# Tanh of a convolved x unit written into its projection's PSUM bank; the tails' B.C copies moved from VectorE to ScalarE

## The chip, the cores and the metric

The kernel runs on one core of one Trainium2 chip. The metric is the device time of one execution in microseconds (us), the median of several runs.

## The reference, cut to what matters

The reference takes x (4 batches of 256 tokens, 512 features) through half an FFN, a Mamba2 mixer, and half an FFN again, each on a layer-normalised input and added back to x. Only the mixer is touched by the change:

```python
proj = hidden_states @ in_proj_w.T
gate, xBC, dt = jnp.split(proj, [INTER, INTER + CONV_DIM], axis=-1)
conv = jax.lax.conv_general_dilated(xBC_t, conv_w, ...)          # causal, 4 taps, by channel
xBC = jax.nn.silu(jnp.swapaxes(conv + conv_b[None, :, None], 1, 2))
x, Bm, Cm = jnp.split(xBC, [INTER, INTER + NG * SS], axis=-1)
scores = jnp.einsum('bclhn,bcshn->bchls', Cc, Bc) * Lmat         # B.C times a decay
Ydiag = jnp.einsum('bchls,bcshp->bclhp', scores, xdt)
yg = y * jax.nn.silu(gate)                                       # then a group RMS norm
return out @ out_proj_w.T
```

INTER is 8192, in NG = 8 groups. A group has its own B and C (128 channels each) and eight x tiles of 128 channels.

## The kernel before, in words

The mixer works group by group (g = 0 to 7). A group has 20 **units**: a unit is one tile of 128 channels (B, C or an x tile) over one half of the 1024 tokens, so 128x512. Units 0 to 3 are B and C, units 4 to 19 the eight x tiles. Each unit passes through five stations:

1. `project` (TensorE, L164 to L166, 12 matmuls of 512 columns) leaves the projection in PSUM bank u % 2.
2. `evacuate` (ScalarE, L955) writes the last tap plus bias from the bank to `acc` in SBUF.
3. `taps` (VectorE, L970, three instructions) read the bank again, shifted, and add to `acc`.
4. `tanh_conv` (ScalarE, L1278) writes tanh of `acc` to the SBUF tile `th`.
5. `silu_conv` (VectorE, L1455) computes `acc = (th + 1) * acc`, with both inputs in SBUF, and raises the semaphore `conv`.

So the bank is free for unit u+2 once the taps of u are done, and that is what `project` waits for. Of the semaphores here, `tap` counts finished taps and `conv` finished `silu_conv`.

The order on every engine is written out by hand: one instruction stream for each, held together by semaphores. A group is eight **pairs** (j = 0 to 7) and a **tail**. In pair j TensorE runs: two transposes of x (L1648), two unit projections, two gate projections (L164 to L166 again, into other banks), two output projections (operand `mx_wo`), and two `mix_tokens` (L1675, L1679). In pair 0 the unit projections (units 6 and 7) come ahead of the transposes. In the first half of group 0 there are no output projections. The tail projects units 2 to 5 of the next group, with the B.C products (`b_dot_c`, L1636, L1637) for each half of the tokens and the sums of squares (L1706) between.

On VectorE a pair has `skip_y` (L1491), `scale_x` (L1480), two `make_mix` (L1473, a decay matrix times `cbt`), the taps of two units, their `silu_conv`, two `silu_gate` (L1497, one input in SBUF, one in PSUM), and `split_wo` (L1501). `cbt` is the SBUF copy of the B.C products. In the tails VectorE copies it (L1462, four instructions of 384 columns for a tail); for group 0 ScalarE does (L1344). GpSimd (POOL) works on SBUF tiles alongside.

Of the kernel before, what the change touches and what calls it, by code (L numbers as in the profile page):

```python
# [28 lines left out]
ALU = mybir.AluOpType  # L29
# [12 lines left out]
TAPS = 4  # L42
# [4 lines left out]
HB = HALF // SEQ  # L47
STEPS = 2 * XT
UNITS = 4 + STEPS
# [4 lines left out]
PAIR = SEQ + CH  # L54
# [767 lines left out]
def first(g):  # L822

    return isinstance(g, int) and g == 0
# [29 lines left out]
def start_at_one(eng, sems):  # L854


    for sem in sems:
        eng.sem_inc(sem, 1)
# [9 lines left out]
class InProj:  # L868
# [51 lines left out]
    def project(self, pe, g, u):  # L920
        nc, m, s = self.nc, self.m, self.s
        w, hf, _ = unit_of(u)
        pe.wait_ge(s["wlo"], 1 + WPG * g + w + 1)
        if not (first(g) and u < 2):
            pe.wait_ge(s["tap"], 1 + (TAPS - 1) * (UNITS * g + u - 1))
        at = slice(hf * HALF, (hf + 1) * HALF)
        for k in range(KT):
            last = three_pass(nc, m.bank[u % 2][:, :], self.w_hi[:, w % 3, k, :], self.w_lo[:, w % 3, k, :],
                              m.h_hi[:, k, at], m.h_lo[:, k, at], k == 0, k == KT - 1)
        last.then_inc(s["proj"], 1)  # L930
# [96 lines left out]
def mixer_phase(nc, m, ip, norm_w, w_out, ncs_dram, next_ln, sums, early):  # L1027

    with ExitStack() as ctx:
# [3 lines left out]
        s, acc, d_raw, w_hi, w_lo = ip.s, ip.acc, ip.d_raw, ip.w_hi, ip.w_lo  # L1033
# [12 lines left out]
        th = sb("th", [P, 2, HALF])  # L1046
        xd = sb("xd", [P, 2, HB * 2, 2, HD])
        mix = sb("mix", [P, 2, 2, HB, PAIR])
        cbt = sb("cbt", [P, 2, HB, PAIR])
# [17 lines left out]
        def step_slot_freed(eng, sem, g, st):  # L1067

            if not (first(g) and st == 0):
                eng.wait_ge(sem, 1 + STEPS * g + st - 1)  # L1070

        def groups_in_turn(pair, tail):

# [184 lines left out]

        @block.scalar
        def _(act):  # L1260
            start_at_one(act, [s["tg"], s["decay"], s["sq"], s["wohi"], s["gcopy"], s["root"]])
            start_after_quad(act, [s["yhi"]])

            def split_wo(g, j):
# [7 lines left out]
            def evacuate(g, u):  # L1272
                ip.evacuate(act, g, u)

            def tanh_conv(g, u):
                act.wait_ge(s["tap"], 1 + (TAPS - 1) * (UNITS * g + u + 1))
                act.wait_ge(s["conv"], 1 + UNITS * g + max(u - 1, 0))
                nc.scalar.activation(th[:, u % 2, :], acc[:, u % 4, :, :].rearrange("p b t -> p (b t)"),  # L1278
                                     ACT.Tanh).then_inc(s["th"], 1)

            def decay_from_first(g, st):

                i, j, hf = st % 2, st // 2, st % 2
                act.wait_ge(s["masked0"], 1 + STEPS * g + st + 1)
                step_slot_freed(act, s["y"], g, st)
                for b in range(HB):
                    for hd in range(2):
                        tile, head = 2 * (HB * hf + b), GH * g + 2 * j + hd
                        nc.scalar.activation(mix[:, i, hd, b, 0:SEQ], csb[:, i, hd, b * SEQ:(b + 1) * SEQ], ACT.Exp,  # L1289
                                             bias=m.ncs[:, tile, head:head + 1], scale=-1.0)  # L1290
# [45 lines left out]
                if n < NG * WPG:  # L1336
                    ip.round_w(act, *weight(n))

            def keep_bc(hf):

                act.wait_ge(s["cb"], 1 + hf + 1)
                banks = Y_BANK if hf == 0 else O_BANK
                for b in range(HB):
                    last = nc.scalar.activation(cbt[:, hf, b, :], banks[b][:, 0:PAIR], ACT.Copy)  # L1344
                last.then_inc(s["cbt"], 1)

            tanh_conv(0, 2)
            keep_bc(0)
            round_w(3)
            tanh_conv(0, 3)  # L1350
            round_w(4)
# [3 lines left out]
            tanh_conv(0, 4)  # L1355
            decay_from_second(0, 0)
            tanh_conv(0, 5)
            keep_bc(1)
            decay_from_first(0, 1)
            decay_from_second(0, 1)  # L1360

# [38 lines left out]
            def tail(g, more):  # L1400
                if more:
                    decay_from_first(g + 1, 0)
                    decay_from_second(g + 1, 0)
                    evacuate(g + 1, 2)
                    square(g, STEPS - 2)
                    round_w(WPG * (g + 1) + 3)
                    evacuate(g + 1, 3)
                    tanh_conv(g + 1, 2)
                    round_tile(g + 1, 0)
                    square(g, STEPS - 1)  # L1410
                    round_w(WPG * (g + 1) + 4)
                    tanh_conv(g + 1, 3)
                    evacuate(g + 1, 4)
                    decay_from_first(g + 1, 1)
                    evacuate(g + 1, 5)
                    tanh_conv(g + 1, 4)
                    decay_from_second(g + 1, 1)
                    round_tile(g + 1, 1)
                    tanh_conv(g + 1, 5)
                else:  # L1420
                    square(g, STEPS - 2)
                    round_tile(NG, 0)
                    square(g, STEPS - 1)
                    keep_first_quad(g, STEPS - 1)
                    for p in range(1, 4):
                        round_tile(NG, p)
                    root(g)
                    for p in range(4, 7):
                        round_tile(NG, p)
                    next_ln.root(act, 0)  # L1430
                    next_ln.normalise(act, 0)
                    next_ln.normalise(act, 1)
                    round_tile(NG, 7)
                    next_ln.normalise(act, 2)
                    next_ln.normalise(act, 3)
                    for t in range(4):
                        next_ln.round(act, t)
                    next_ln.root(act, 1)
# [2 lines left out]

        @block.vector
        def _(dve):
            start_at_one(dve, [s["mix"], s["xd"], s["sg"], s["ysb"], s["cbt"],
                               s["ms"], s["inv"], s["wolo"]])
            start_after_quad(dve, [s["gsum"], s["outsb"]])

# [3 lines left out]
            def silu_conv(g, u):  # L1451

                dve.wait_ge(s["th"], 1 + UNITS * g + u + 1)
                a = acc[:, u % 4, :, :].rearrange("p b t -> p (b t)")
                nc.vector.scalar_tensor_tensor(a, th[:, u % 2, :], 1.0, a, ALU.add, ALU.mult).then_inc(s["conv"], 1)  # L1455

            def keep_bc(g, hf):
                dve.wait_ge(s["cb"], 1 + 2 * g + hf + 1)
                dve.wait_ge(s["mix"], 1 + STEPS * g)
                banks = Y_BANK if hf == 0 else O_BANK  # L1460
                for b in range(HB):
                    last = nc.vector.tensor_copy(cbt[:, hf, b, :], banks[b][:, 0:PAIR])  # L1462
                last.then_inc(s["cbt"], 1)

            def make_mix(g, st):

# [104 lines left out]
            def tail(g, more):  # L1571
                skip_y(g, STEPS - 2)
                skip_y(g, STEPS - 1)
                if more:
                    head_constants(g + 1)
                    taps(g + 1, 2)
                    taps(g + 1, 3)
                    silu_conv(g + 1, 2)
                    silu_conv(g + 1, 3)
                    taps(g + 1, 4)  # L1580
                    taps(g + 1, 5)
                    mean_square(g)
                    silu_conv(g + 1, 4)
                    silu_conv(g + 1, 5)
                    keep_bc(g + 1, 0)
                    keep_bc(g + 1, 1)
                else:
                    add_quads(NG, 0)
                    add_quads(NG, 1)
                    mean_square(g)  # L1590
                    inverse(g)
                    add_group(NG, 0)
                    add_group(NG, 1)
                    for n in (2, 3):
                        add_quads(NG, n)
                        add_group(NG, n)
                    add_quads(NG, 4)
                    for n in range(4):
                        sums.wait(dve, NG, n)
                        next_ln.statistics(n)  # L1600
                    next_ln.variances(dve, 0)
                    add_group(NG, 4)
                    next_ln.scales(dve, 0)
                    add_quads(NG, 5)
                    add_group(NG, 5)
                    for n in (4, 5):
                        sums.wait(dve, NG, n)
                        next_ln.statistics(n)
                    add_quads(NG, 6)
                    add_group(NG, 6)  # L1610
                    next_ln.remainder(dve, 0)
                    sums.wait(dve, NG, 6)
                    next_ln.statistics(6)
                    next_ln.variances(dve, 1)
                    for t in range(1, 4):
                        next_ln.remainder(dve, t)
                    next_ln.scales(dve, 1)
# [195 lines left out]
```

## Time and profile before

| what | value |
|---|---|
| median of 3 runs | 1576.83 us (1575.9 to 1577.28) |
| the profiled execution | 1575.93 us |
| its span, first to last instruction | 1573.7 us |
| TensorE (PE) busy | 1529.4 us, 97% of the span |
| VectorE (DVE) busy | 1367.7 us, 87% |
| ScalarE (ACT) busy | 1010.5 us, 64% |
| GpSimd (POOL) busy | 1045.9 us, 66% |
| granted TensorE clock | 0.993 of full |

The profiled execution has 2.2 us around its span. PE is TensorE, PEld its weight loads, which overlap the matmuls. An engine's idle time counts only where another engine, in the end TensorE, is kept waiting by it.

### The profile page before, as it was taken

What the parts mean: (1) busy time and instruction counts of PE and PEld (TensorE: products, weight loads), DVE (VectorE), ACT (ScalarE), POOL (GpSimd) and SP (SyncE); (2) the same over time, 40 slices, a digit from 0 to 9 for tenths busy, and PEclk for the clock granted to TensorE, in tenths of its full rate; (3) what the DMA queues carried; (4) which work ended last, traced back from release to release, by engine and by line L of the source; (5) the groups of instructions that cost most, each with busy time, mean ns of one, the idle gap of its engine ahead of it and who ended that gap; (6) DMA issues with size and microseconds to landing.
All of it is one profiled execution on the core that took longest, in us unless ns stands there. A gap on an engine that the chain in (4) does not pass through costs nothing. (4 is left out here: it accounts for less than half of the span.)

```text
span 1573.7 us, 24488 instructions
## 1 busy us (share of the span) xinstructions
PE 1529.4 (97%) x8296; PEld 1229.0 (78%) x8296; DVE 1367.7 (87%) x1676; ACT 1010.5 (64%) x2126; POOL 1045.9 (66%) x789
## 2 busy tenths in 40 slices
PE   6978999999999999999999999999999999999988
PEld 4766788788888888788888888788888888788766
DVE  6679988998889988998889988998889988998674
ACT  4467766667666667667666667666666677567641
POOL 3026887588757887588757887488757886588740
PEclk9989999999999999999999999999999999999999
DMA  3033332223222232233222332223223322222101
GB/s 122 1 105 110 101 95 75 84 92 95 86 71 93 94 95 74 81 94 96 81 74 95 95 95 74 81 94 95 81 75 94 94 95 74 81 94 81 59 17 53
DMA packets 73514, 131.62 MB, mean 84 GB/s; under 512 B 10800, under 2 KB 10800, under 8 KB 73136
## 3 DMA queue, kind: packets, MB, share of 16 engines
q1 hardware_dynamic: 73392, 130.07, 25.9%
q8 instruction: 67, 1.10, 0.3%
q14 instruction: 55, 0.45, 0.1%
HBM read 127.43 MB, written 2.62 MB: 83 GB/s over the span
## 5 line engine op out<-in xcount | busy, mean ns | idle before, releaser
L164 PE MATMUL bank<-h_hi,mx_w_hi 128*128 128x512 f32 x1152 | 457.5, 397 | 5.1 <-DVE mx_xd L1480 4.0
L166 PE MATMUL bank<-h_hi,mx_w_lo 128*128 128x512 f32 x1152 | 449.5, 390 | 0.0
L165 PE MATMUL bank<-h_lo,mx_w_hi 128*128 128x512 f32 x1152 | 448.4, 389 | 0.0
L970 DVE SCALAR_TENSOR_TENSOR mx_acc<-bank,mx_cw,mx_acc 128x510 f32<-128x510 f32 (+2 forms) x480 | 353.7, 745 | 55.4 <-ACT mx_acc L955 43.9
L1289 ACT ACTIVATE mx_mix<-mx_csb,ncs 128x256 f32<-128x256 f32 x512 | 217.9, 497 | 138.5 <-PE bank L1679 138.5
L1473 DVE TENSOR_TENSOR mx_mix<-mx_mix,mx_cbt 128x1536 f32<-128x1536 f32 x128 | 280.5, 2196 | 2.5 <-ACT mx_mix L1299 2.5
L917 POOL TENSOR_TENSOR mx_w_lo<-mx_w_raw,mx_w_hi 128x512 fp32r<-128x512 f32 x144 | 213.8, 1501 | 74.3 <-ACT mx_w_hi L912 74.1
L164 PEld LDWEIGHTS bank<-h_hi,mx_w_hi 128*128 128x128 f32 x1152 | 216.5, 188 | 50.9 <-issue 8.7
L166 PEld LDWEIGHTS bank<-h_hi,mx_w_lo 128*128 128x128 f32 x1152 | 216.3, 188 | 46.3
L1200 POOL TENSOR_TENSOR mx_ssum<-mx_ssum,mx_sq 128x512 f32<-128x512 f32 x112 | 216.3, 1954 | 51.5 <-ACT mx_sq L1321 51.5
L165 PEld LDWEIGHTS bank<-h_lo,mx_w_hi 128*128 128x128 f32 x1152 | 216.7, 188 | 42.7
L1192 POOL TENSOR_TENSOR mx_yt_lo<-mx_y,mx_yt_hi 128x512 fp32r<-128x512 f32 x128 | 213.2, 1681 | 39.2 <-ACT mx_yt_hi L1312 39.1
L1455 DVE SCALAR_TENSOR_TENSOR mx_acc<-mx_th,mx_acc 128x512 f32<-128x512 f32 x158 | 229.2, 1450 | 4.0 <-ACT mx_th L1278 3.2
L1187 POOL TENSOR_TENSOR mx_y<-mx_y,mx_sg 128x512 f32<-128x512 f32 x128 | 201.4, 1594 | 13.0 <-DVE mx_y L1491 13.0
L164 PE MATMUL bank<-mx_wo_hi,mx_yt_hi 128*128 128x512 f32 x512 | 200.9, 392 | 1.3 <-POOL mx_yt_lo L1192 1.3
L166 PE MATMUL bank<-mx_wo_hi,mx_yt_lo 128*128 128x512 f32 x512 | 200.2, 391 | 0.0
L955 ACT ACTIVATE mx_acc<-bank,mx_cb,mx_cw 128x512 f32<-128x512 f32 x160 | 124.4, 779 | 117.8 <-PE bank L166 101.3
L165 PE MATMUL bank<-mx_wo_lo,mx_yt_hi 128*128 128x512 f32 x512 | 199.2, 389 | 0.0
L1172 POOL TENSOR_SCALAR_AFFINE_SELECT mx_csb<-mx_csb 128x512 f32<-128x512 f32 x128 | 110.5, 864 | 133.2 <-DMA mx_csb<-cs_rows 133.2
L1179 POOL TENSOR_SCALAR_AFFINE_SELECT mx_mix<-mx_csb 128x512 f32<-128x512 f32 x128 | 87.9, 690 | 145.7 <-PE bank L1679 145.6
L1299 ACT ACTIVATE mx_mix<-mx_mix,ncs 128x128 f32<-128x128 f32 x512 | 162.3, 389 | 7.7 <-POOL mx_mix L1179 7.6
L1675 PE MATMUL bank<-mx_mix,mx_xd 128*64 128x256 f32 x1024 | 157.3, 386 | 0.0
(171 smaller groups left out, 2132.6 us busy)
## 6 DMA issues: line engine op xcount, KB each, us to landing
mx_csb<-cs_rows SPq DMA_DIRECT2D x128, 512.0 KB, 3.9
mx_w_raw<-in_w_in SPq DMA_DIRECT2D x144, 256.0 KB, 2.9
mx_wo_raw<-in_w_out SPq DMA_DIRECT2D x64, 256.0 KB, 4.1
res<-in_x SPq DMA_DIRECT2D x8, 256.0 KB, 4.8
out<-res SPq DMA_DIRECT2D x8, 256.0 KB, 2.0
f_base_raw<-in_base_wt SPq DMA_DIRECT2D x1, 1024.0 KB, 7.4
mx_acc<-in_base_wt SPq DMA_DIRECT2D x1, 1024.0 KB, 4.8
cs_rows<-f_xn SPq DMA_DIRECT2D x2, 256.0 KB, 2.0
```

What stands on the lines that cost most here:

```text
L164: nc.tensor.matmul(out, w_hi, x_hi, start=first, stop=False)
L165: nc.tensor.matmul(out, w_hi, x_lo, start=False, stop=False)
L166: return nc.tensor.matmul(out, w_lo, x_hi, start=False, stop=last)
L917: self.nc.gpsimd.tensor_tensor(self.w_lo[:, w % 3, :, :], self.w_raw[:, w % 3, :, :], self.w_hi[:, w % 3, :, :].bitcast(F32), ALU.subtract ...
L970: self.nc.vector.scalar_tensor_tensor(dst, src[:, :, 0:SEQ - k], self.cw[:, c, TAPS - 1 - k:TAPS - k], dst, ALU.mult, ALU.add).then_inc(s[ ...
L1187: nc.gpsimd.tensor_tensor(y[:, st, :], y[:, st, :], sg[:, st % 2, :], ALU.mult).then_inc(s["yg"], 1)
L1192: nc.gpsimd.tensor_tensor(yt_lo[:, p % 2, :, :], y_tile(q, hf, t), yt_hi[:, p % 2, :, :].bitcast(F32), ALU.subtract).then_inc(s["ylo"], 1)
L1200: nc.gpsimd.tensor_tensor(ssum[:, i, :], ssum[:, i, :], sq[:, i, :], ALU.add).then_inc(s["ssum"], 1)
L1289: nc.scalar.activation(mix[:, i, hd, b, 0:SEQ], csb[:, i, hd, b * SEQ:(b + 1) * SEQ], ACT.Exp, bias=m.ncs[:, tile, head:head + 1], scale=-1.0)
L1299: last = nc.scalar.activation(mix[:, i, hd, b, SEQ:PAIR], mix[:, i, hd, b, SEQ:PAIR], ACT.Exp, bias=m.ncs[:, tile, head:head + 1], scale=-1.0)
L1455: nc.vector.scalar_tensor_tensor(a, th[:, u % 2, :], 1.0, a, ALU.add, ALU.mult).then_inc(s["conv"], 1)
L1473: nc.vector.tensor_tensor(a, a, both, ALU.mult).then_inc(s["mix"], 1)
```

## The change

For units 0, 1 and 4 to 19 of a group the tanh goes to the unit's own PSUM bank, which the taps have finished reading, instead of to `th`; `silu_conv` reads it there. Units 2 and 3 keep `th`. A bank that holds a tanh is free only after the `silu_conv` that reads it, so `project` waits for `conv` of unit u-2 instead of `tap`, except for units 4 and 5 (and units 2 and 3 of group 0). The copies of the B.C products in the tails go from VectorE's stream to ScalarE's, the first ahead of `decay_from_first(g + 1, 1)`, the second at the end of the tail, and `decay_from_second(g + 1, 1)` moves behind the last tanh.

```diff
@@ project
         if not (first(g) and u < 2):
-            pe.wait_ge(s["tap"], 1 + (TAPS - 1) * (UNITS * g + u - 1))
+            if 4 <= u < 6 or (first(g) and u < 4):
+                pe.wait_ge(s["tap"], 1 + (TAPS - 1) * (UNITS * g + u - 1))
+            else:
+                pe.wait_ge(s["conv"], 1 + UNITS * g + u - 1)
...
+        def tanh_place(u):
+
+            return m.bank[u % 2][:, :] if u < 2 or u >= 4 else th[:, u % 2, :]
@@ scalar: tanh_conv
-                nc.scalar.activation(th[:, u % 2, :], acc[:, u % 4, :, :].rearrange("p b t -> p (b t)"),
+                nc.scalar.activation(tanh_place(u), acc[:, u % 4, :, :].rearrange("p b t -> p (b t)"),
                                      ACT.Tanh).then_inc(s["th"], 1)
@@ scalar: keep_bc
-            def keep_bc(hf):
-
-                act.wait_ge(s["cb"], 1 + hf + 1)
+            def keep_bc(g, hf):
+
+                act.wait_ge(s["cb"], 1 + 2 * g + hf + 1)
+                act.wait_ge(s["mix"], 1 + STEPS * g)
@@ scalar: tail
                     evacuate(g + 1, 4)
+                    keep_bc(g + 1, 0)
                     decay_from_first(g + 1, 1)
                     evacuate(g + 1, 5)
                     tanh_conv(g + 1, 4)
-                    decay_from_second(g + 1, 1)
                     round_tile(g + 1, 1)
                     tanh_conv(g + 1, 5)
+                    decay_from_second(g + 1, 1)
+                    keep_bc(g + 1, 1)
@@ vector: silu_conv
-                nc.vector.scalar_tensor_tensor(a, th[:, u % 2, :], 1.0, a, ALU.add, ALU.mult).then_inc(s["conv"], 1)
+                nc.vector.scalar_tensor_tensor(a, tanh_place(u), 1.0, a, ALU.add, ALU.mult).then_inc(s["conv"], 1)
@@ vector: tail
                     silu_conv(g + 1, 4)
                     silu_conv(g + 1, 5)
-                    keep_bc(g + 1, 0)
-                    keep_bc(g + 1, 1)
```

How it stands on the engines. On TensorE, from the second B.C product of the first tail into `project` of unit 6, which opens pair 0 of group 1; before:

```order
L1636 MATMUL bank<-mx_acc 128x256 [waits mx_gcopy,mx_conv]
L1637 MATMUL bank<-mx_acc 128x128
L1636 MATMUL bank<-mx_acc 128x256
L1637 MATMUL bank<-mx_acc 128x128
L164 MATMUL bank<-h_hi,mx_w_hi 128x512 [waits mx_tap,mx_wlo]
L165 MATMUL bank<-h_lo,mx_w_hi 128x512
```

and now:

```order
L1636 MATMUL bank<-mx_acc 128x256 [waits mx_gcopy,mx_conv]
L1637 MATMUL bank<-mx_acc 128x128
L1636 MATMUL bank<-mx_acc 128x256
L1637 MATMUL bank<-mx_acc 128x128
L164 MATMUL bank<-h_hi,mx_w_hi 128x512 [waits mx_conv,mx_wlo]
L165 MATMUL bank<-h_lo,mx_w_hi 128x512
```

The order of the matmuls is the same; only the semaphore of unit 6's first matmul has changed. (Lines in the order of the changed kernel carry that file's own numbers; TensorE's happen to be the same in both.)

On ScalarE, the end of the same tail, from `evacuate` of unit 4 to the rounding of the next weight (`mx_w_hi`); before:

```order
L955 ACTIVATE mx_acc<-bank,mx_cb,mx_cw 128x512
L1289 ACTIVATE mx_mix<-mx_csb,ncs 128x256 x4
L955 ACTIVATE mx_acc<-bank,mx_cb,mx_cw 128x512
L1278 ACTIVATE mx_th<-mx_acc 128x512
L1299 ACTIVATE mx_mix<-mx_mix,ncs 128x128 x4
L1312 ACTIVATE mx_yt_hi<-mx_y 128x512
L1278 ACTIVATE mx_th<-mx_acc 128x512
L912 ACTIVATE mx_w_hi<-mx_w_raw 128x512
```

and now:

```order
L958 ACTIVATE mx_acc<-bank,mx_cb,mx_cw 128x512
L1352 ACTIVATE mx_cbt<-bank 128x384 x2
L1296 ACTIVATE mx_mix<-mx_csb,ncs 128x256 x4
L958 ACTIVATE mx_acc<-bank,mx_cb,mx_cw 128x512
L1285 ACTIVATE bank<-mx_acc 128x512
L1319 ACTIVATE mx_yt_hi<-mx_y 128x512
L1285 ACTIVATE bank<-mx_acc 128x512
L1306 ACTIVATE mx_mix<-mx_mix,ncs 128x128 x4
L1352 ACTIVATE mx_cbt<-bank 128x384 x2
L912 ACTIVATE mx_w_hi<-mx_w_raw 128x512
```

Two copies now stand between the evacuations of units 4 and 5, and two more and the four decays of L1306 behind the tanh of unit 5.

On VectorE, the same place, from the last tap of unit 5 to `make_mix` of the next group; before:

```order
L970 SCALAR_TENSOR_TENSOR mx_acc<-bank,mx_cw,mx_acc 128x2x253
L1509 TENSOR_SCALAR mx_rms<-bank 128x8
L1455 SCALAR_TENSOR_TENSOR mx_acc<-mx_th,mx_acc 128x512 x2
L1462 COPY mx_cbt<-bank 128x384 x4
L1480 TENSOR_TENSOR mx_xd<-bank,mx_gdt 128x512 x2
L1473 TENSOR_TENSOR mx_mix<-mx_mix,mx_cbt 128x1536 x2
```

and now:

```order
L973 SCALAR_TENSOR_TENSOR mx_acc<-bank,mx_cw,mx_acc 128x2x253
L1511 TENSOR_SCALAR mx_rms<-bank 128x8
L1465 SCALAR_TENSOR_TENSOR mx_acc<-bank,mx_acc 128x512 x2
L1482 TENSOR_TENSOR mx_xd<-bank,mx_gdt 128x512 x2
L1475 TENSOR_TENSOR mx_mix<-mx_mix,mx_cbt 128x1536 x2
```

The four copies are gone, and the two `silu_conv` (units 4 and 5) take a bank as an input; they still stand behind the taps of unit 5 and `mean_square` (L1511).

## Rows read from the trace of the kernel before

**Rows 1.** Page, part 1: busy us (share of the span) xinstructions.

```profile
PE 1529.4 (97%) x8296; PEld 1229.0 (78%) x8296; DVE 1367.7 (87%) x1676; ACT 1010.5 (64%) x2126; POOL 1045.9 (66%) x789
```

**Rows 2.** TensorE's waits: who waited for whom, us in total, times, longest.

```profile
PE bank L1648 <- DVE mx_sg L1497: 6.2, 7, 2.2
...
PE bank L164 <- DVE mx_xd L1480: 4.0, 9, 0.5
```

**Rows 3.** Groups of VectorE instructions: busy us, mean ns | idle before.

```profile
L1455 DVE SCALAR_TENSOR_TENSOR mx_acc<-mx_th,mx_acc 128x512 f32<-128x512 f32 x158 | 229.2, 1450 | 4.0 <-ACT mx_th L1278 3.2
...
L1497 DVE SCALAR_TENSOR_TENSOR mx_sg<-mx_sg,bank 128x512 f32<-128x512 f32 x128 | 86.4, 676 | 0.0
```

**Rows 4.** Timeline of TensorE, end of the first tail: start us, us.

```profile
267.35 1.84 PE L1706 MATMUL bank<-ones,mx_ssum 128*128 128x1 f32 x16
...
270.36 0.48 PE L164 MATMUL bank<-h_hi,mx_w_hi 128*128 128x512 f32 x1
...
277.37 0.47 PE L164 MATMUL bank<-h_hi,mx_w_hi 128*128 128x512 f32 x1 [0.44 <-DVE mx_xd L1480]
```

**Rows 5.** Timeline of VectorE in the same tail (two windows of it).

```profile
266.12 4.55 DVE L970 SCALAR_TENSOR_TENSOR mx_acc<-bank,mx_cw,mx_acc 128x510 f32<-128x510 f32 x6
270.59 0.16 DVE L1509 TENSOR_SCALAR mx_rms<-bank 128x8 f32<-128x8 f32 x1
270.66 0.68 DVE L1455 SCALAR_TENSOR_TENSOR mx_acc<-mx_th,mx_acc 128x512 f32<-128x512 f32 x1
...
272.97 1.94 DVE L1462 COPY mx_cbt<-bank 128x384 f32<-128x384 f32 x4
276.53 1.29 DVE L1480 TENSOR_TENSOR mx_xd<-bank,mx_gdt 128x512 f32<-128x512 f32 x2 [1.62 <-PE bank L1648]
277.74 3.85 DVE L1473 TENSOR_TENSOR mx_mix<-mx_mix,mx_cbt 128x1536 f32<-128x1536 f32 x2
```

**Rows 6.** Timeline of ScalarE in the same tail.

```profile
264.82 0.78 ACT L955 ACTIVATE mx_acc<-bank,mx_cb,mx_cw 128x512 f32<-128x512 f32 x1 [0.29 <-PE bank L166]
265.50 1.69 ACT L1289 ACTIVATE mx_mix<-mx_csb,ncs 128x256 f32<-128x256 f32 x4
267.55 0.78 ACT L955 ACTIVATE mx_acc<-bank,mx_cb,mx_cw 128x512 f32<-128x512 f32 x1 [0.35 <-PE bank L166]
...
273.38 0.78 ACT L955 ACTIVATE mx_acc<-bank,mx_cb,mx_cw 128x512 f32<-128x512 f32 x1 [1.52 <-PE bank L166]
```

**Rows 7.** Windows: length; busy us of PE, PEld, DVE, ACT, POOL; clock, DMA share, GB/s.

```profile
255.06:277.37 22.31, 21.87 (x112) 18.48 (x113) 18.18 (x26) 15.54 (x32) 14.38 (x11) 1.00 0.29 95
...
1320.27:1342.58 22.31, 21.87 (x113) 18.49 (x113) 18.19 (x26) 15.55 (x32) 14.39 (x11) 1.00 0.28 91
120.00:180.00 60.00, 53.81 (x326) 42.22 (x323) 58.46 (x66) 44.94 (x100) 41.89 (x36) 1.00 0.33 103
```

**Rows 8.** Timelines of TensorE, VectorE and ScalarE, start of group 0.

```profile
107.17 0.47 PE L164 MATMUL bank<-h_hi,mx_w_hi 128*128 128x512 f32 x1 [0.66 <-DVE mx_acc L970]
...
109.20 0.68 DVE L1455 SCALAR_TENSOR_TENSOR mx_acc<-mx_th,mx_acc 128x512 f32<-128x512 f32 x1
...
114.54 4.53 DVE L1473 TENSOR_TENSOR mx_mix<-mx_mix,mx_cbt 128x1536 f32<-128x1536 f32 x2
...
109.86 0.85 ACT L1344 ACTIVATE mx_cbt<-bank 128x384 f32<-128x384 f32 x2
110.60 1.70 ACT L1289 ACTIVATE mx_mix<-mx_csb,ncs 128x256 f32<-128x256 f32 x4
```

**Rows 9.** Groups of VectorE instructions from 130 to 175 us.

```profile
L1455 DVE SCALAR_TENSOR_TENSOR mx_acc<-mx_th,mx_acc 128x512 f32<-128x512 f32 x6 | 7.0, 1170 | 0.0
```

**Rows 10.** Timeline of TensorE: transposes of the second half, group 0.

```profile
142.04 0.63 PE L1648 MATMUL bank<-ident,mx_acc 128*128 128x128 f32 x4 [0.94 <-DVE mx_sg L1497]
...
158.35 0.63 PE L1648 MATMUL bank<-ident,mx_acc 128*128 128x128 f32 x4 [1.05 <-DVE mx_sg L1497]
...
174.70 0.63 PE L1648 MATMUL bank<-ident,mx_acc 128*128 128x128 f32 x4 [1.06 <-DVE mx_sg L1497]
```

More of the change, by code:

```diff
@@ L1260, in _ @@
         def _(act):
-            start_at_one(act, [s["tg"], s["decay"], s["sq"], s["wohi"], s["gcopy"], s["root"]])
+            start_at_one(act, [s["cbt"], s["tg"], s["decay"], s["sq"], s["wohi"], s["gcopy"], s["root"]])
             start_after_quad(act, [s["yhi"]])
@@ L1347, in _ @@
             tanh_conv(0, 2)
-            keep_bc(0)
+            keep_bc(0, 0)
             round_w(3)
@@ L1357, in _ @@
             tanh_conv(0, 5)
-            keep_bc(1)
+            keep_bc(0, 1)
             decay_from_first(0, 1)
@@ L1443, in _ @@
         def _(dve):
-            start_at_one(dve, [s["mix"], s["xd"], s["sg"], s["ysb"], s["cbt"],
+            start_at_one(dve, [s["mix"], s["xd"], s["sg"], s["ysb"],
                                s["ms"], s["inv"], s["wolo"]])
@@ L1454, in silu_conv @@
                 a = acc[:, u % 4, :, :].rearrange("p b t -> p (b t)")
-                nc.vector.scalar_tensor_tensor(a, th[:, u % 2, :], 1.0, a, ALU.add, ALU.mult).then_inc(s["conv"], 1)
[L1457 to L1463, printed above, removed]
+                nc.vector.scalar_tensor_tensor(a, tanh_place(u), 1.0, a, ALU.add, ALU.mult).then_inc(s["conv"], 1)
             def make_mix(g, st):
```

## The prediction

> **What bounds the kernel now.** I read the shares of busy time first: TensorE is busy for 97% of the span and VectorE for 87% [rows 1]. So a microsecond saved on VectorE is worth something only where TensorE stands still for it. The list of TensorE's waits says where that is: inside the mixer it lost 6.2 us to `silu_gate` ahead of the transposes (L1648), and 4.0 us, in nine pieces of at most 0.5, to `scale_x` ahead of a gate projection [rows 2]. The 6.2 us all lie in the first half of group 0: from 120 to 180 us VectorE was busy for 58.46 of 60 us and TensorE for 53.81, and the transposes there wait about 1 us a pair [rows 7, 10]. That is the only stretch that VectorE bounds. From then on TensorE runs without gaps, the tails included: 21.87 of 22.31 us in the first and in the last of seven [rows 7]. What it misses there is the one wait for `scale_x`, 0.44 us [rows 4], and `scale_x` had itself waited 1.62 us for TensorE's transpose [rows 5]. That pause is the way there and back, and no freed VectorE time shortens it.
>
> So I ask two things. How much of the 6.2 us does the change return? And does it put a new wait in front of TensorE where it has none now?
>
> **The new wait.** `project` of unit u now waits for `silu_conv` of unit u-2 instead of its taps. In pairs 1 to 7 this costs nothing: the transposes just ahead of the two projections already wait for the same two `silu_conv`. In the tails units 2 and 3 wait for units 0 and 1, finished within pair 7, ahead of its output projections; units 4 and 5 keep the old wait. There remains pair 0, where the projections come first. Unit 6 must wait for `silu_conv` of unit 4, and that stands on VectorE behind the taps of unit 5 and `mean_square`.
>
> In the first tail unit 6 starts at 270.36 [rows 4]. `silu_conv` of unit 4 starts at 270.66 and takes 0.68 [rows 5]: it begins after TensorE now goes past. From its end to the first matmul I take 0.16: `scale_x` starts at 276.53, 0.68 for it as for such an operation (half of the two is 0.65) gives 277.21, and the matmul that waits for it starts at 277.37 [rows 4, 5]. So unit 6 could start at 270.66 + 0.68 + 0.16 = 271.50, 1.14 us later than now, with nothing else changed.
>
> The moved copies add to that. Two copies on ScalarE take 0.74 us from the first to the next operation (109.86 to 110.60) [rows 8]. They now stand between the evacuations of units 4 and 5, where ScalarE idles for 0.35 us [rows 6], so the evacuation of unit 5 slips by 0.39. It ends at 267.55 + 0.78 = 268.33, and the taps of unit 5 are the second half of the six that start at 266.12 and take 4.55, so they start near 268.40 [rows 5, 6]. The cover is 0.07 at most. The slip therefore goes through to `silu_conv` with 0.32 to 0.39, and the wait is 1.46 to 1.53 us; I take 1.5.
>
> Nothing takes it back. What queues behind unit 6 on TensorE is unit 7, the transposes and all the rest; `scale_x` follows the transposes, and TensorE has no later gap to absorb it. Unit 7 does not wait a second time: `silu_conv` of unit 5 ends some 0.8 us behind that of unit 4, and unit 6 itself takes 2.8. The seven tails read alike [rows 7], so **7 x 1.5 = +10.5 us**.
>
> In group 0 the same wait stands ahead of unit 6: it starts at 107.17, `silu_conv` of unit 4 at 109.20 [rows 8]. 109.20 + 0.68 + 0.16 - 107.17 = **+2.9**. Part comes back: two `make_mix` at 114.54 took 4.53 us, against 3.85 for the two after the first tail [rows 5, 8], because POOL's work fell on them; 2.9 us later most of that is done. I take **-0.5** of the 0.68 (bounds: 0 and 0.7).
>
> **What the bank as an input saves.** `silu_conv` has a mean of 1450 ns, `silu_gate`, the same operation with one input from a bank, 676 ns [rows 3], and `silu_conv` itself 0.68 where nothing disturbs it [rows 5]. So the price is 0.68, and at most 0.76 (a tap, which also reads a bank and `acc`, 4.55 / 6 [rows 5]). 142 of 158 change, so VectorE is relieved of 142 x 0.77 = 109 us, and of seven times 1.94 us of copies. Nearly all of it falls where VectorE waits for TensorE, and is worth nothing. In the bound stretch, six `silu_conv` take 7.0 us, 1170 ns each [rows 9]; at 0.68 they take 4.1. VectorE's chain there shortens by 2.9, about 1 us a pair, just under the 1 us that the transposes wait in a pair [rows 10], so TensorE gets nearly all: **-2.9** (bounds: 0, if POOL's freed work falls on another VectorE operation, and 6.2, all the waits).
>
> The Trainium skill (Perfetto Trace Analysis, Optimizing Scalar/DVE Operations) gives VectorE about 60 ns of access overhead per operation on SBUF and about 125 on PSUM. By it an undisturbed `silu_conv` would become some 65 ns longer, an estimate from that page, and the sum about 0.8 us larger (thirteen operations on the path). The rows do not show it: 676 ns with a bank, 680 without.
>
> **What costs nothing.** Tanh written to a bank has no row here. With bounds of nothing and the 0.78 of an evacuation it stays off the path: unit 4's tanh has over 1 us until its `silu_conv`, unit 5's is wanted 2.8 us later. The second pair of copies and the moved decays stand ahead of the evacuation of unit 6, where ScalarE idled for 1.52 us [rows 6] and which itself comes 1.5 later. Uncovered, the 0.74 would delay that evacuation alone. VectorE's freed copies leave it waiting for the transpose, as it did already.
>
> **The sum.** 10.5 + 2.9 - 0.5 - 2.9 = +10.0 us. Against the profiled execution, span 1573.7 + 10.0 = 1583.7, and 2.2 around it, 1585.9. That execution was 0.9 below the median of 1576.83, so the median should be **1586.8 us**, 0.6% slower. Within 0.2%, 3.2 us, a measurement of this kernel can't tell from no change.
>
> **Rivals.**
> - *Faster.* VectorE's time is the price of group 0, and the tails are covered. If all 6.2 us returned and unit 6 of group 0 cost 2.4, group 0 would give 3.8; with no wait in the tails that is 1573.0. It takes a wait under 0.1 us a tail. Against it: six taps from 266.12, 4.55 long, end at 270.6 [rows 5], after 270.36, and `silu_conv` stands behind them. The skill's same section says that moving work from a saturated VectorE to ScalarE may make sense; by that rule this rival wins, but only 60 us here are so bound. Chance 0.04.
> - *No change.* The wait is met earlier, or absorbed by the 0.44 us pause and group 0's return. To stay within 3.2 us it takes under 0.6 us a tail, half of the 1.14 that stands without any slip; about 1578. Chance 0.05.
> - *Slower, but the copies fit.* Evacuations come no later, the wait is 1.14: 8.0 - 0.5 = +7.5, 1584.3. It needs copies of 0.35 us for both; they take 0.74. Chance 0.13.
> - *Slower, and group 0 returns nothing.* With 0.76 for `silu_conv`: 7 x 1.6 + 2.9 = 14.1, 1590.9. For it speaks that POOL works all through that stretch, 41.89 of 60 us [rows 7]. Chance 0.08.
>
> My forecast has 0.70, between 1584 and 1590. Its low bounds (1.14 a tail, all of group 0's 6.2 back) come to 8.0 + 2.4 - 6.2 = +4.2, near 1581, the high ones to 1590.9. I give 1582 to 1591. Slower by over 0.2%: 0.70 + 0.13 + 0.08 = 0.91; same 0.05; faster 0.04.
>
> **What would show it.** TensorE's waits: a new one for `silu_conv` ahead of unit 6, eight times, 1.2 to 1.5 us in the tails and nearly 3 in group 0; the 6.2 us for `silu_gate` down to 2 to 4. `silu_conv` near 0.75 us in the mean, VectorE below 1260 us busy. The evacuation of unit 5 0.3 to 0.4 us later behind unit 5's last matmul. I am wrong if unit 6 of a tail starts at its old distance of 3.0 us behind the sums of squares (267.35 to 270.36 [rows 4]), or if TensorE has new gaps inside the pairs.

## Result, and the profile after

The changed kernel took 1589.12 us (median of 6 executions, 1583.17 to 1589.54), the kernel before 1577.39 beside it (1575.9 to 1577.84). The ratio is 1.0065, 95% interval 1.0048 to 1.0083: slower by 0.65%. The prediction was 1586.8, in a range of 1582 to 1591. The profiled execution took 1584.3 us with a span of 1582.3, 8.6 above the span before.

VectorE was relieved as planned; page, part 1 (columns as in [rows 1]):

```profile
PE 1533.2 (97%) x8296; PEld 1231.0 (78%) x8296; DVE 1243.1 (79%) x1648; ACT 1018.8 (64%) x2154; POOL 1008.2 (64%) x789
```

VectorE fell from 87 to 79%, TensorE stayed at 97%. The groups of `silu_conv` (now L1465) and of the tanh (L1285), busy us and mean ns of one:

```profile
L1465 DVE SCALAR_TENSOR_TENSOR mx_acc<-bank,mx_acc 128x512 f32<-128x512 f32 x142 | 96.6, 680 | 0.1
...
L1285 ACT ACTIVATE bank<-mx_acc 128x512 f32<-128x512 f32 x142 | 83.6, 589 | 59.4 <-DVE mx_acc L973 59.3
...
L1465 DVE SCALAR_TENSOR_TENSOR mx_acc<-mx_th,mx_acc 128x512 f32<-128x512 f32 x16 | 18.4, 1152 | 4.3 <-ACT mx_th L1285 3.8
...
L1285 ACT ACTIVATE mx_th<-mx_acc 128x512 f32<-128x512 f32 x16 | 10.0, 626 | 2.1 <-DVE mx_acc L973 2.1
```

With a bank as input `silu_conv` takes 680 ns, as the rows of `silu_gate` had suggested [rows 3]; the sixteen that still read `th` take 1152. TensorE's waits, in us, times and longest, show what came in exchange:

```profile
PE bank L164 <- DVE mx_acc L1465: 11.0, 8, 2.8
...
PE bank L164 <- DVE mx_xd L1482: 4.0, 9, 0.5
...
PE bank L1648 <- DVE mx_sg L1499: 2.4, 4, 1.1
```

The wait for `silu_gate` shrank from 6.2 to 2.4 us, and a wait of 11.0 us for `silu_conv` is new, eight times: once in group 0 and at the end of each of the seven tails. TensorE's timeline at the end of the first tail:

```profile
266.09 1.84 PE L1706 MATMUL bank<-ones,mx_ssum 128*128 128x1 f32 x16
...
270.52 0.47 PE L164 MATMUL bank<-h_hi,mx_w_hi 128*128 128x512 f32 x1 [1.17 <-DVE mx_acc L1465]
...
277.52 0.47 PE L164 MATMUL bank<-h_hi,mx_w_hi 128*128 128x512 f32 x1 [0.44 <-DVE mx_xd L1482]
```

Unit 6 starts 4.43 us behind the sums of squares (270.52 - 266.09), where it was 3.01 [rows 4]. The other six tails read 4.42 or 4.43 too, so each lost 1.42 us. The list of waits has 1.17 of that; the rest is that before, unit 6 started 0.24 us ahead of the modelled end of the matmul in front of it (270.60). The 0.44 us for `scale_x` is unchanged. VectorE's and ScalarE's timelines of the same tail say why:

```profile
264.86 2.30 DVE L973 SCALAR_TENSOR_TENSOR mx_acc<-bank,mx_cw,mx_acc 128x510 f32<-128x510 f32 x3
267.39 2.31 DVE L973 SCALAR_TENSOR_TENSOR mx_acc<-bank,mx_cw,mx_acc 128x510 f32<-128x510 f32 x3 [0.24 <-ACT mx_acc L958]
269.62 0.16 DVE L1511 TENSOR_SCALAR mx_rms<-bank 128x8 f32<-128x8 f32 x1
269.69 1.37 DVE L1465 SCALAR_TENSOR_TENSOR mx_acc<-bank,mx_acc 128x512 f32<-128x512 f32 x2
276.69 1.29 DVE L1482 TENSOR_TENSOR mx_xd<-bank,mx_gdt 128x512 f32<-128x512 f32 x2 [5.62 <-PE bank L1648]
```

```profile
263.57 0.78 ACT L958 ACTIVATE mx_acc<-bank,mx_cb,mx_cw 128x512 f32<-128x512 f32 x1 [0.29 <-PE bank L166]
264.25 0.86 ACT L1352 ACTIVATE mx_cbt<-bank 128x384 f32<-128x384 f32 x2
264.99 1.70 ACT L1296 ACTIVATE mx_mix<-mx_csb,ncs 128x256 f32<-128x256 f32 x4
266.59 0.78 ACT L958 ACTIVATE mx_acc<-bank,mx_cb,mx_cw 128x512 f32<-128x512 f32 x1
...
273.53 0.78 ACT L958 ACTIVATE mx_acc<-bank,mx_cb,mx_cw 128x512 f32<-128x512 f32 x1 [0.72 <-PE bank L166]
```

The two copies (L1352) now stand between the evacuations of units 4 and 5. The second evacuation starts without idle time, 0.50 us behind the start of the sums of squares (before: 267.55 against 267.35, 0.20 [rows 4, 6]), so 0.30 late. VectorE's second set of taps now waits 0.24 us for it, and `silu_conv` of unit 4 follows at 269.69, 3.60 us behind the sums of squares instead of 3.31 [rows 4, 5]. TensorE waits for just that. VectorE then sits idle for 5.62 us until the transposes, where it had idled for 1.62 [rows 5]: what it saved became waiting.

In group 0 the same wait, on TensorE and VectorE:

```profile
109.97 0.47 PE L164 MATMUL bank<-h_hi,mx_w_hi 128*128 128x512 f32 x1 [2.77 <-DVE mx_acc L1465]
...
112.77 0.39 PE L164 MATMUL bank<-h_hi,mx_w_hi 128*128 128x512 f32 x1
```

```profile
109.14 1.44 DVE L1465 SCALAR_TENSOR_TENSOR mx_acc<-bank,mx_acc 128x512 f32<-128x512 f32 x2
...
117.34 3.42 DVE L1475 TENSOR_TENSOR mx_mix<-mx_mix,mx_cbt 128x1536 f32<-128x1536 f32 x2
```

Unit 6 starts 2.80 us later than before [rows 8]. TensorE's wait itself grew only from 0.66 to 2.77: the other 0.69 stood ahead of it, since in this execution the granted clock was still low at unit 4 (0.62 from 99 to 103 us, before 0.87), whose twelve matmuls took 4.48 us instead of 3.31. Unit 6 did not start later for that: VectorE came to `silu_conv` of unit 4 at 109.14, before at 109.20.

The two `make_mix` take 3.42 us instead of 4.53, and the first transposes of pair 1 wait less. Before, then now:

```profile
124.86 0.63 PE L1648 MATMUL bank<-ident,mx_acc 128*128 128x128 f32 x4 [2.24 <-DVE mx_sg L1497]
```

```profile
126.54 0.63 PE L1648 MATMUL bank<-ident,mx_acc 128*128 128x128 f32 x4 [1.13 <-DVE mx_sg L1499]
```

Then the pairs catch up; from 120 to 180 us TensorE is busy for 57.65 us (PE is the first column behind the length; [rows 7] had 53.81), and the transposes wait 0.33 us where they waited 1.06 [rows 10]:

```profile
120.00:180.00 60.00, 57.65 (x343) 45.34 (x342) 58.42 (x69) 46.08 (x103) 41.47 (x36) 1.00 0.35 110
```

```profile
172.46 0.66 PE L1648 MATMUL bank<-ident,mx_acc 128*128 128x128 f32 x4
173.45 0.63 PE L1648 MATMUL bank<-ident,mx_acc 128*128 128x128 f32 x4 [0.33 <-DVE mx_sg L1499]
173.83 0.48 PE L164 MATMUL bank<-h_hi,mx_w_hi 128*128 128x512 f32 x1
```

The last of these is the first projection of pair 4, which before started later:

```profile
175.08 0.48 PE L164 MATMUL bank<-h_hi,mx_w_hi 128*128 128x512 f32 x1
```

### The profile page after: what moved, and what is told of

Read it like the earlier page. It is cut to its first block and busy times, and to the rows that moved or that the text cites. A ratio compares the mean times of both kernels' runs of the same rounds, so it can differ in the third digit from the quotient of the medians.

```text
span 1582.3 us, 24490 instructions
## 1 busy us (share of the span) xinstructions
PE 1533.2 (97%) x8296; PEld 1231.0 (78%) x8296; DVE 1243.1 (79%) x1648; ACT 1018.8 (64%) x2154; POOL 1008.2 (64%) x789
## 5 line engine op out<-in xcount | busy, mean ns | idle before, releaser
L1475 DVE TENSOR_TENSOR mx_mix<-mx_mix,mx_cbt 128x1536 f32<-128x1536 f32 x128 | 267.2, 2093 | 2.4 <-ACT mx_mix L1306 2.4
L917 POOL TENSOR_TENSOR mx_w_lo<-mx_w_raw,mx_w_hi 128x512 fp32r<-128x512 f32 x144 | 203.7, 1432 | 101.9 <-ACT mx_w_hi L912 101.7
L1194 POOL TENSOR_TENSOR mx_y<-mx_y,mx_sg 128x512 f32<-128x512 f32 x128 | 233.1, 1842 | 9.6 <-DVE mx_y L1493 9.5
L1199 POOL TENSOR_TENSOR mx_yt_lo<-mx_y,mx_yt_hi 128x512 fp32r<-128x512 f32 x128 | 178.6, 1413 | 31.4 <-ACT mx_yt_hi L1319 31.2
L1493 DVE SCALAR_TENSOR_TENSOR mx_y<-mx_acc,mx_dh,bank 128x512 f32<-128x512 f32 x128 | 94.5, 745 | 125.3 <-PE bank L1679 125.2
L1179 POOL TENSOR_SCALAR_AFFINE_SELECT mx_csb<-mx_csb 128x512 f32<-128x512 f32 x128 | 88.1, 689 | 131.6 <-DMA mx_csb<-cs_rows 131.6
L1306 ACT ACTIVATE mx_mix<-mx_mix,ncs 128x128 f32<-128x128 f32 x512 | 162.3, 389 | 5.1 <-POOL mx_mix L1186 4.9
```

Of the source, the lines that this page charges most:

```text
L917: self.nc.gpsimd.tensor_tensor(self.w_lo[:, w % 3, :, :], self.w_raw[:, w % 3, :, :], self.w_hi[:, w % 3, :, :].bitcast(F32), ALU.subtract ...
L1194: nc.gpsimd.tensor_tensor(y[:, st, :], y[:, st, :], sg[:, st % 2, :], ALU.mult).then_inc(s["yg"], 1)
L1199: nc.gpsimd.tensor_tensor(yt_lo[:, p % 2, :, :], y_tile(q, hf, t), yt_hi[:, p % 2, :, :].bitcast(F32), ALU.subtract).then_inc(s["ylo"], 1)
L1306: last = nc.scalar.activation(mix[:, i, hd, b, SEQ:PAIR], mix[:, i, hd, b, SEQ:PAIR], ACT.Exp, bias=m.ncs[:, tile, head:head + 1], scale=-1.0)
L1475: nc.vector.tensor_tensor(a, a, both, ALU.mult).then_inc(s["mix"], 1)
```

## Experiments

The theory: the loss is the wait of unit 6 for `silu_conv` of unit 4 and nothing else, lengthened by the place of the first copies; the gain is confined to group 0. Rivals: the copies on ScalarE, or the bank's use as such, cost TensorE time. A second question came with the result. Executions of the same changed kernel lay at 1583 to 1584 us with a mean granted clock of 0.994, or at 1589 with 0.990, where the kernel before had 0.991 to 0.994. All times below stand beside executions of the kernel before on the same chip (1575.9 to 1577.4 in the median).

**e1: the change again**, unedited.

> The changed kernel once more. The theory (unit 6 of a group waits for silu_conv of unit 4): 7.5 to 9.5 us above the kernel before where the clock is granted as in the profile of after, each tail 1.4 us longer from the sums of squares to unit 6 (4.4 instead of 3.0). Its other executions were some 5 us longer at a mean granted clock of 0.990 instead of 0.994; if such a one is profiled, the theory expects the same 4.4 in every tail and the extra time in one stretch of low clock near the start. Rival (the tails' delay varies from run to run): the extra 5 us would lie in the tails, 0.7 each.

Ratio 1.0067 (1.0052 to 1.0082), four executions from 1584.82 to 1589.51. The profiled one had 0.994 and 4.42 to 4.44 us in all tails. It fits, 9.0 us above the span before; two of the others were at 0.990, but none of those was profiled. For that see e12.

**e2: units 4 and 5 in `th`**, so units 6 and 7 wait for taps again.

```diff
-            if 4 <= u < 6 or (first(g) and u < 4):
+            if 4 <= u < 8 or (first(g) and u < 4):
...
-            return m.bank[u % 2][:, :] if u < 2 or u >= 4 else th[:, u % 2, :]
+            return m.bank[u % 2][:, :] if u < 2 or u >= 6 else th[:, u % 2, :]
```

> Units 4 and 5 keep th too, so units 6 and 7 wait for taps again; the copies stay on ScalarE and the other units use the bank. The theory: the wait in the tails is gone (unit 6 again 3.0 us behind the sums of squares), the copies' slip is hidden because only unit 7 waits for the taps of unit 5 and that has 2 us of room; group 0 keeps its saving of 2.9 us. 2 to 4 us faster than before, 11 to 13 faster than the change. Rival one (the copies on ScalarE cost TensorE time): 2 us or more lost in the tails, so no faster than before. Rival two (tanh in a bank slows TensorE or ScalarE by itself): slower than before.

1574.82 us, ratio 0.9986 (0.9976 to 0.9995): faster than before, and 13 us faster than the change beside it. TensorE in the first tail:

```profile
266.84 1.84 PE L1706 MATMUL bank<-ones,mx_ssum 128*128 128x1 f32 x16
...
269.86 0.48 PE L164 MATMUL bank<-h_hi,mx_w_hi 128*128 128x512 f32 x1
```

3.02 us, as before the change, with the copies on ScalarE and 126 of the 142 tanhs still in banks. Both rivals fall here.

**e3: the wait alone**, in the kernel before: `project` gets the change's waits, tanh stays in `th`, the copies on VectorE.

> The kernel before with the changed wait alone: project waits for silu_conv as in the change, tanh stays in th and the copies on VectorE. The theory: 1.14 us in each tail (8.0 in all), and in group 0 2.9 less about 1.1 that make_mix gives back because POOL is done by then, and nothing saved in the pairs: 9 to 10.5 us slower than before. Rival (the copies or the bank cause the loss, not the wait): within 1 us of before.

1589.02 us, ratio 1.0073 (1.0054 to 1.0093): as slow as the change, from an edit that moves no work at all. That is 11.6 us, above the 9 to 10.5 that I expected. The span of its profile is 12.4 above the one before; 3.1 of these lie behind two falls of the clock, at unit 8 of group 0 (its twelve matmuls took 4.44 us instead of 2.85) and in the last FFN (4.42 instead of 2.88), and without them it is 9.3. The first tail:

```profile
270.27 1.84 PE L1709 MATMUL bank<-ones,mx_ssum 128*128 128x1 f32 x16
...
274.41 0.47 PE L164 MATMUL bank<-h_hi,mx_w_hi 128*128 128x512 f32 x1 [0.88 <-DVE mx_acc L1458]
```

4.14 us in every tail, so 1.13 of wait without the copies; the prediction had 1.14 for that.

**e4: the copies alone** (with the moved decays), the change with every tanh in `th` and all the old waits.

```diff
-            if 4 <= u < 6 or (first(g) and u < 4):
-                pe.wait_ge(s["tap"], 1 + (TAPS - 1) * (UNITS * g + u - 1))
-            else:
-                pe.wait_ge(s["conv"], 1 + UNITS * g + u - 1)
+            pe.wait_ge(s["tap"], 1 + (TAPS - 1) * (UNITS * g + u - 1))
...
-            return m.bank[u % 2][:, :] if u < 2 or u >= 4 else th[:, u % 2, :]
+            return th[:, u % 2, :]
```

> The changed kernel with every tanh in th and the old waits for taps: only the copies go to ScalarE. The theory: the evacuation of unit 5 comes 0.3 to 0.4 us later and nothing waits for it, so within 1 us of before. Rival (the slip reaches TensorE by itself): 7 x 0.3 = 2 us slower or more.

1577.16 us, ratio 1.0 (0.999 to 1.0009), 3.01 to 3.02 us in the tails. The slip of the evacuation costs only where TensorE waits for what follows it.

**e5 and e6: the wait in group 0 alone, and in the tails alone.** `tanh_place` gets g as well, and units 4 and 5 use their banks only where `first(g)` holds (e5), or only where it doesn't (e6); units 6 and 7 wait for taps where units 4 and 5 use `th`.

```diff
-            if 4 <= u < 6 or (first(g) and u < 4):
+            if 4 <= u < 6 or (first(g) and u < 4) or (u in (6, 7) and not (first(g))):
...
-            return m.bank[u % 2][:, :] if u < 2 or u >= 4 else th[:, u % 2, :]
+            in_bank = u < 2 or u >= 6 or (u >= 4 and first(g))
+            return m.bank[u % 2][:, :] if in_bank else th[:, u % 2, :]
```

> The change, but units 4 and 5 use their banks in group 0 only; in the seven tails they use th and units 6 and 7 wait for taps. The theory: the tails cost nothing (3.0 us from the sums of squares to unit 6); group 0 pays 2.8 for its wait and gets 1.1 (make_mix) and 2.9 (silu_conv) back, so some 1 us faster than before at the same granted clock. Question of the clock: if the executions of the change at a mean clock of 0.990 come from TensorE's 2.8 us wait at 107 us, they appear here too, 3 to 5 us above the others; if they come from the tails, all runs here lie at 0.991 to 0.994 as for the kernel before.

> The opposite: units 4 and 5 use their banks in the seven tails only, and th in group 0. The theory: 7 x 1.42 = 9.9 us in the tails, group 0 without its wait gains 2.9, so 6 to 8 us slower than before. Clock: if the wait in group 0 makes the executions at 0.990, they are absent here.

e5: 1579.44 us, ratio 1.0011 (1.0001 to 1.0021). The tails read 3.0. Of ten executions three lay at 1574.3 to 1576.1 with a clock of 0.993, seven at 1579 to 1580 with 0.990. So in the median it is 0.11% slower, where the sum at an even clock gave some 1 us faster; only the three at 0.993 lie below the 1576.68 of the kernel before. e6: 1582.78, ratio 1.0045 (1.003 to 1.006); the tails read 4.43, and no execution was at 0.990. So the seven tails cost what the theory says, and the executions at 0.990 go with the wait in group 0.

**e7 and e8: the copies back on VectorE** (the lines of the diff on the copies undone), **and the first copies later on ScalarE** (the diff is that of e8):

```diff
                     evacuate(g + 1, 4)
-                    keep_bc(g + 1, 0)
                     decay_from_first(g + 1, 1)
                     evacuate(g + 1, 5)
                     tanh_conv(g + 1, 4)
+                    keep_bc(g + 1, 0)
```

> The change with the tails' copies back on VectorE, behind the two silu_conv as before. The theory: ScalarE evacuates unit 5 without the slip, so the tails' wait is 1.13 instead of 1.42: 2 us faster than the change in the profile's span, 4.14 instead of 4.43 us from the sums of squares to unit 6. Rival (the copies belong to VectorE's end of the tail and hold TensorE there): 1.9 us of copies lengthen each tail, slower than the change.

> The change with the first copy of a tail on ScalarE moved behind the evacuation and the tanh of unit 4 and 5's evacuation, still on ScalarE. The theory: what costs is the place ahead of the evacuation of unit 5, not the engine: 4.14 us from the sums of squares to unit 6 in every tail, as with the copies on VectorE. Rival (ScalarE's work in the tail is too long as such): it stays at 4.43.

e7: 1585.8 us, ratio 1.0057 (1.004 to 1.0074); e8 took 1583.23 in its one execution. In both the tails read 4.13 to 4.14. For e8 in the first tail:

```profile
268.66 1.84 PE L1706 MATMUL bank<-ones,mx_ssum 128*128 128x1 f32 x16
...
272.80 0.47 PE L164 MATMUL bank<-h_hi,mx_w_hi 128*128 128x512 f32 x1 [0.88 <-DVE mx_acc L1465]
```

So 1.13 us of a tail's loss is the wait and 0.29 the copies' place ahead of the evacuation on ScalarE; later on ScalarE (e8) or on VectorE (e7) they add nothing. The span of e7 did not come out 2 us below that of the change, as I had expected, but 2.8 above it, 1585.1 us. About 2 us were won in the tails; 3.1 were lost ahead of the first, and 1.6 in the last FFN. Half of the 3.1 lies before the mixer, the other half at unit 6 of group 0:

```profile
111.08 0.47 PE L164 MATMUL bank<-h_hi,mx_w_hi 128*128 128x512 f32 x1 [3.40 <-DVE mx_acc L1463]
...
115.50 0.40 PE L164 MATMUL bank<-h_hi,mx_w_hi 128*128 128x512 f32 x1
```

The twelve matmuls of unit 6 took 4.42 us there behind the wait; in the profile of the change they took 2.80 (112.77 - 109.97).

**e9, e10, e11: TensorE kept busy in the waits of group 0.** Extra matmuls, whose results nothing reads, run while TensorE would wait ahead of unit 6 and ahead of the transposes of pair 1: ten and four in the change (e9), three and eight in e2 (e10), two and eight in the kernel before (e11).

```diff
+            def fill(bank, n):
+                for _ in range(n):
+                    nc.tensor.matmul(bank[:, :], m.h_hi[:, 0, 0:P], m.h_hi[:, 0, 0:HALF], start=True, stop=True)
+
+            fill(TG_BANK[1], 10)
...
+                if g == 0 and j == 1:
+                    pe.wait_ge(s["cbt"], 3)
+                    fill(O_BANK[0], 4)
```

> The change with TensorE kept busy in its two long waits of group 0: ten extra matmuls of 512 columns (2.3 us) into an idle bank while unit 6 waits 2.8 us, and four (0.9 us) ahead of the transposes of pair 1. The extra matmuls compute nothing that is used. The clock theory: the drops of the granted clock behind these waits (unit 6 taking 4.42 us instead of 2.80, unit 8 taking 4.45 instead of 2.85) are gone, no execution lies at 0.990, and the median falls to 1582 to 1585 us; the tails still read 4.43. Rival (the 0.990 has another cause, in the FFN phases): the times spread as for the change, up to 1589.

> The version with units 4 and 5 in th, and TensorE kept busy with three extra matmuls ahead of unit 6 and eight ahead of the transposes of pair 1, in group 0. It wrote 1572 to 1576.6 us without them, the drop of clock behind the transposes seen in its profile. The clock theory: the upper half of these executions goes, median 1572 to 1574. Rival: as without, 1574.8.

> Control: the kernel before with two extra matmuls ahead of unit 6 and eight ahead of the transposes of pair 1 of group 0, nothing else. The clock theory: 1 to 2 us faster than before in the median, since some of its executions (0.991 to 0.992) would lose the drop behind the transposes; never slower. If it is as fast as the version with units 4 and 5 in th, the gain of that version would be one of the clock and not of the bank.

e9: 1587.02 us, ratio 1.0063 (1.0049 to 1.0076), 1584.31 to 1587.9 with clocks of 0.992 to 0.994. The executions at 0.990 are gone and the highest is 1.6 us lower, but the median is 2 us above what I expected, and its ratio is, within the intervals, that of the change (1.0065). In its profile the clock (third column from the right) holds at 1.00 around both waits:

```profile
108.00:112.00 4.00, 2.52 (x12) 1.79 (x11) 2.56 (x4) 3.55 (x11) 0.00 (x0) 1.00 0.36 113
112.00:116.00 4.00, 4.00 (x21) 3.33 (x20) 0.00 (x0) 2.88 (x8) 1.88 (x2) 1.00 0.05 19
128.00:132.00 4.00, 4.00 (x20) 3.21 (x20) 3.29 (x6) 3.03 (x10) 4.00 (x5) 1.00 0.21 66
132.00:136.00 4.00, 4.00 (x19) 3.31 (x18) 3.93 (x4) 4.00 (x10) 3.51 (x3) 1.00 0.55 197
```

Yet this profile's span is 1.7 us longer than that of the profile of after (1584.0 against 1582.3). Up to unit 6 of the last group TensorE stands within 0.1 us of it; 1.6 are lost in the last FFN, where twelve matmuls took 4.41 us instead of 2.84 at a lower clock:

```profile
1538.00:1542.00 4.00, 2.35 (x7) 1.86 (x7) 3.06 (x9) 1.81 (x4) 2.20 (x2) 0.72 0.01 4
1542.00:1546.00 4.00, 4.00 (x21) 3.32 (x20) 0.00 (x0) 1.24 (x3) 0.00 (x0) 0.85 0.00 0
```

e10: 1573.48 us, ratio 0.9981 (0.9973 to 0.999), the fastest version found by its median, with the upper executions of e2 (1576.6) gone; the intervals of e10 and e2 overlap, so that it beats e2 is not shown. e11: 1576.49, ratio 0.9999 (0.999 to 1.0008): no gain, against my 1 to 2 us, though its clock was 0.993 to 0.994 in all executions. The gain of e2 and e10 is therefore the bank's, in group 0, and not the clock's: from the transposes of pair 1 to the first projection of pair 4 the profile of e10 gains 2.95 us on the one before, that of e11 nothing.

**e12: the change a third time**, one execution with its profile.

> The changed kernel a third time, for one more profile. Clock theory: if this execution is one at a mean clock of 0.990 to 0.991 (1586 to 1590 us), unit 6 or unit 8 of group 0 takes 4.4 us instead of 2.8 behind TensorE's waits there; if it lies at 0.994 (1583 to 1585 us), neither does. In both the tails read 4.43. Rival: a time near 1589 with both at 2.8, the extra time elsewhere.

1591.01 us at 0.990. TensorE at units 6 and 7 of group 0, then windows of 4 us (same columns as [rows 7]):

```profile
112.61 0.76 PE L164 MATMUL bank<-h_hi,mx_w_hi 128*128 128x512 f32 x1 [3.76 <-DVE mx_acc L1465]
...
116.81 0.40 PE L164 MATMUL bank<-h_hi,mx_w_hi 128*128 128x512 f32 x1
```

```profile
108.00:112.00 4.00, 0.84 (x6) 0.60 (x4) 3.86 (x7) 3.42 (x10) 0.35 (x1) 1.00 0.42 125
112.00:116.00 4.00, 3.39 (x9) 2.76 (x10) 1.15 (x2) 4.00 (x12) 0.00 (x0) 0.57 0.42 131
116.00:120.00 4.00, 4.00 (x22) 3.28 (x20) 0.00 (x0) 1.58 (x4) 1.88 (x2) 1.00 0.18 65
128.00:132.00 4.00, 2.13 (x24) 1.38 (x20) 3.93 (x7) 2.90 (x7) 0.56 (x1) 1.00 0.00 0
132.00:136.00 4.00, 3.77 (x12) 2.97 (x13) 3.35 (x6) 3.04 (x9) 4.00 (x5) 0.58 0.23 66
136.00:140.00 4.00, 4.00 (x19) 3.29 (x18) 3.57 (x4) 2.70 (x7) 3.62 (x2) 1.00 0.61 181
```

Unit 6 waits 3.76 us and its matmuls then take 4.20 us instead of 2.80; the granted clock is 0.57 from 112 to 116 us, that is mostly at the lower level, 1.2 instead of 2.4 GHz. It falls again behind the transposes' wait at 131 us: 0.58, and unit 8 takes 4.36 us instead of 2.85. Together 2.9 us of the 6.9 by which this span exceeds that of the profile of after. About 2 more came before the mixer's first matmul, and 1.6 from twelve matmuls of the last FFN that took 4.42 us instead of 2.84. Both places are outside the change, and the 1.6 is no sign of the wait: the same twelve matmuls took 4.4 us in the profiles of e2, which has no such wait, and of e9. The tails read 4.42 to 4.43.

## Why the prediction was right

By its steps:

- **What bounds.** Right. TensorE had no slack from group 1 on, so 125 us less work on VectorE (1367.7 to 1243.1) returned nothing there; e2 and e10 show the return of group 0 by itself.
- **The new wait in the tails.** Predicted 1.5 us, seven times, 10.5; measured 1.42, 9.9. Its two parts were measured apart: 1.13 for `silu_conv` (predicted 1.14; e3, e7, e8) and 0.29 for the copies' place (predicted 0.32 to 0.39). I had taken the slip as what of the copies the idle time of 0.35 does not hold; the evacuation came 0.30 late, since the rows of ScalarE overlap by some 0.1 us (the decays end at 264.99 + 1.70 = 266.69, the evacuation starts at 266.59), so there was more room than the idle time showed.
- **The wait in group 0.** Predicted 2.9, measured 2.80. The part that `make_mix` gives back was mis-sized: 0.5 taken, 1.1 measured. Unit 6 came 2.80 us late, the first transposes of pair 1 only 1.68 (126.54 against 124.86). Before, a POOL operation ran beside the two `make_mix` from 115.31 to 117.46; now POOL idles from 115.88 to 119.95. That POOL is the cause is read from this overlap and was not tested apart. I had capped the return at 0.68, from a pair of `make_mix` that itself had POOL beside it (1.37 us from 278.62).
- **The saving of `silu_conv` in group 0.** Predicted 2.9. Between those transposes and the first projection of pair 4 TensorE went from 1.68 behind to 1.25 ahead (173.83 against 175.08), so 2.93. In the same stretch the seven `silu_conv` took 4.8 us instead of 7.7, and VectorE's other groups moved by 0.3 at most.
- **A bank as input costs VectorE nothing.** 680 ns with it; an undisturbed one had taken 680 without. The Trainium skill (Perfetto Trace Analysis, Optimizing Scalar/DVE Operations) would have had it some 65 ns longer, an estimate from its 60 and 125 ns; here no run shows that.
- **The sum.** In the two profiles, at mean clocks of 0.993 and 0.994, +10.0 predicted and +8.6 measured in the spans. Right in sign and mechanism, large by the `make_mix` term and the slip.
- **What was left out.** Nothing in my sum let a wait of TensorE cost more than its own length. In some executions the granted clock fell behind the wait of unit 6 or that of the transposes, and the matmuls behind each lost some 1.5 us more (e7, e12). This lifts the median above the sum, and 1589 is nearer to my range's upper end than to its middle by the clock, not by a longer wait. That the median came within 2.3 us of the forecast is in part luck: the sum was 1.4 too large, and the clock added some 5 us in four of six executions. None of the six lies near 1586.8.

The faster rival fell as it was argued: unit 6 would have had to start before `silu_conv` of unit 4 does. The rival in which the copies fit is what e8 shows, at 1.13 a tail; in the change they did not fit, by 0.29. The rival in which group 0 returns nothing fell: it returned 1.1 and 2.9.

What stays open is why the clock falls in some executions and not in others, behind the same wait. In those with the wait in group 0 (the change, e1, e3, e5, e7, e8, e12) 16 of 30 were at 0.990; in those without it (e2, e4, e6) none of 24, nor any of the kernel before, nor any of the five of e9, where TensorE works through the first part of the wait (1.48 us of it are left). That ties 0.990 to that wait, though of the extra time of e12 only 2.9 us lie behind the waits of group 0. Its length alone does not settle it: behind unit 6 the clock held after 2.77 us (after) and 3.30 (e3) and fell after 3.40 (e7), 3.58 (e8) and 3.76 (e12), but behind the transposes of pair 1 it fell after 1.13 us in e3 and held after 1.56 in e7, and after a wait of 2.2 us there it fell in e2 and held in e4 and the kernel before. One thing goes with the outcome at unit 6: where the clock held (after, e1, e3, e5), unit 4 had still run mostly at the lower clock, 4.38 to 4.51 us for its twelve matmuls; where it fell (e7, e8, e12), unit 4 had taken 3.33 to 3.51. Why is not shown. Nor is it shown why the executions of e9 that were not profiled stand above my expectation.

## What to carry to other kernels

Before an intermediate is parked in the buffer that the bounding engine writes next, look up what that buffer's release turns into: here "the last reader is done" became "the reader's reader is done", and it cost wherever the producer runs right behind, in one unit out of twenty. Work taken off an engine counts only in the stretch that the engine bounds; find that stretch in the list of waits and price the change there, with the new wait priced everywhere. When a scheme is right for most units, give the few at the seam their old place: two units back in `th` turned 0.65% slower into 0.14% faster, and 0.19% with TensorE kept busy in group 0 (the two intervals overlap).

## What the runs showed of the hardware

- Behind waits of TensorE in group 0 the granted clock fell from 2.4 GHz to the lower level for a few us, in some executions only, and twelve matmuls then took 4.2 to 4.45 us instead of 2.8. With ten matmuls that compute nothing in the wait it stayed at 1.00 there in the profile of e9. The last FFN shows the same two speeds, 2.84 or 4.42 us for twelve matmuls, in kernels with the wait and without it.
- ScalarE's tanh took 589 ns into a bank against 626 into SBUF, for the same input in SBUF. The Trainium skill (ScalarE: Activation LUTs, Step-by-step: what each stage is for) says that writing to PSUM is the faster way; the rows agree, by 6%.
- `silu_conv` with both inputs in SBUF took 0.68 us or up to 1.8, 1450 ns in the mean [rows 3]: 679 to 694 ns in the 11 that no POOL operation overlaps, up to 1821 in the 147 that one does. With one input in a bank the 142 lay between 676 and 692 ns, 125 of them with a POOL operation beside them.
